# Where the rows of the links and the slot positions are loaded in a two-layer graph kernel

## The reference

```python
src = concatenate([src0, arange(n)]); dst = concatenate([dst0, arange(n)])
h = x @ w_in + b_in
for l in range(2):
    xn = layernorm(h, ln1_g[l], ln1_b[l])
    q, k, v = (xn @ w[l] + b[l] for w, b in ((wq, bq), (wk, bk), (wv, bv)))   # 8 heads of 32
    scores = einsum("ehd,ehd->eh", q[dst], k[src]) * 32 ** -0.5
    ex = exp(scores - segment_max(scores, dst)[dst])
    attn = ex / segment_sum(ex, dst)[dst]
    agg = segment_sum(attn[:, :, None] * v[src], dst)
    h = h + agg @ wo[l] + bo[l]
    h = h + gelu(layernorm(h, ln2_g[l], ln2_b[l]) @ w1[l] + b1[l]) @ w2[l] + b2[l]
x = x + h                                  # h was computed from layernorm(x)
# then: route the mean token to 2 of 8 experts, x = x + layernorm(experts(layernorm(x)) + layernorm(x))
```

## Time and profile before

| | us |
|---|---|
| median of 3 runs | 3951.3 |
| lowest, highest | 3948.37, 3951.6 |
| the profiled execution, its own time | 3945.3 |
| its span | 3943.5 |
| TensorE busy | 2343.8 (59%) |
| VectorE busy | 2487.8 (63%) |
| GpSimd busy | 1835.6 (47%) |

### The profile page before, as it was taken

One profiled execution on the slowest core, in us unless ns is written; L12 is line 12 of the kernel. 1 busy time (PEld: TensorE's weight loads), 2 busy tenths in 40 slices (PEclk: granted clock), 3 DMA queues, 4 the chain that ended last, 5 costly groups with the idle time before them and its releaser, 6 DMA issues. The chain is left out here.

```text
span 3943.5 us, 37530 instructions
## 1 busy us (share of the span) xinstructions
PE 2343.8 (59%) x7257; PEld 1553.1 (39%) x7258; DVE 2487.8 (63%) x3969; ACT 1326.8 (34%) x3895; POOL 1835.6 (47%) x1938
## 2 busy tenths in 40 slices
PE   5763455555455555568882555545555555478798
PEld 3331333333233333345551333333333333256576
DVE  3653677787777777734333777777777877544433
ACT  1112344444344343312112443444444434222131
POOL 4005566666666666311006666666666666211000
PEclk8776676666766676679995766676776666689899
DMA  3225667677677666522216767667666766412111
GB/s 91 64 69 175 186 206 210 203 212 213 201 210 209 207 205 205 154 63 78 72 53 192 211 203 213 205 203 209 207 210 204 212 208 211 118 54 66 39 37 33
DMA packets 293357, 623.34 MB, mean 158 GB/s; under 512 B 51905, under 2 KB 163705, under 8 KB 293184
## 3 DMA queue, kind: packets, MB, share of 16 engines
q0 software_dynamic: 149904, 471.38, 40.8%
q1 hardware_dynamic: 143280, 150.27, 12.0%
HBM read 526.62 MB, written 94.78 MB: 158 GB/s over the span
## 5 line engine op out<-in xcount | busy, mean ns | idle before, releaser
L725 POOL DMA_INDIRECT ring<-kv_table,stage_ix x1760 | 1672.9, 951 | 987.9 <-issue 591.4
L951 PE MATMUL bank<-qs,hot_q 128*128 x1760 | 716.2, 555 | 638.3 <-issue 328.0
L964 PE MATMUL bank<-ring,hot_w 128*128 128x272 f32 x1760 | 704.3, 540 | 501.8 <-issue 295.6
L1860 DVE TENSOR_TENSOR ring<-ring,bank 128x1024 f32<-128x1024 f32 x440 | 532.6, 1210 | 548.9 <-issue 309.5
L951 PEld LDWEIGHTS bank<-qs,hot_q 128*128 128x128 f32 x1760 | 462.4, 275 | 819.9 <-issue 723.9
L964 PEld LDWEIGHTS bank<-ring,hot_w 128*128 128x128 f32 x1760 | 421.1, 259 | 768.5 <-issue 494.4
L1865 DVE TENSOR_REDUCE s<-ring 128x32 f32<-128x1024 f32 x440 | 532.8, 1211 | 4.2
L1210 ACT ACTIVATE stage_o<-bank 128x272 f32<-128x272 f32 x440 | 167.3, 385 | 507.4 <-remote 334.5
L1195 ACT ACTIVATE s<-bank 128x8 f32<-128x8 f32 x440 | 78.0, 177 | 728.5 <-remote 449.1
L1185 ACT ACTIVATE hot_q<-pos_b,row_of 128x128 f32<-128x128 bf16 x880 | 304.0, 395 | 6.8 <-issue 3.4
L1877 DVE TENSOR_TENSOR bank<-ring,bank 128x512 f32<-128x512 f32 x440 | 300.9, 684 | 0.0
(11 more groups left out here) (298 smaller groups left out, 2348.7 us busy)
## 6 DMA issues: line engine op xcount, KB each, us to landing
agg_d<-stage_o SPq DMA_DIRECT2D x440, 136.0 KB
ring<-kv_table,stage_ix POOLq DMA_INDIRECT x1760
pos_b<-rel_d SPq DMA_DIRECT2D x54, 256.0 KB
kv_table<-ring SPq DMA_DIRECT2D x50, 250.0 KB
h_dram<-ring SPq DMA_DIRECT2D x15, 625.0 KB
ring<-h_dram SPq DMA_DIRECT2D x15, 625.0 KB
q_tab<-ring SPq DMA_DIRECT2D x10, 644.5 KB
ring<-in_x_dram SPq DMA_DIRECT2D x10, 625.0 KB
```

Source lines behind the costliest of these rows:

```text
L725: gps.indirect_dma_start(out=chunk[:, par * G + i, j, :], out_offset=None, in_=table, in_offset=bass.IndirectOffsetOnAxis(ap=stage_ix[:, p ...
L951: mm = ten.matmul(q_bank(third, i)[:, 0:QC], hot_q[:, i % 4, a * P:(a + 1) * P], qs[:, bass.ds(t * QC + a * QC, QC)], start=(a == 0), stop ...
L964: mm = ten.matmul(b_acc[i % 2][:, lo - OWN:MC], hot_w[:, i % 4, :], chunk[:, s, j, lo:ROW], start=(j == 0), stop=(j == QD // 2 - 1), skip_ ...
L1860: tt(k_, k_, q, ALU.mult).then_inc(S["q_used"], 1)
```

## The change

Three things are moved, all on SyncE, and nothing else is altered:

- behind `edges(0)` the first rows (`firsts(0)`, with its four waits) are loaded ahead of the 16 weight loads instead of behind them;
- behind `edges(1)` the same with `firsts(1)` and the 8 weight loads;
- the positions of groups 0 and 1 for layer 1 are no longer loaded behind `edges(0)`, but at the beginning of SyncE's last batch of the middle stage.

```diff
--- before.py
+++ after.py
@@ -524,6 +524,9 @@
 
                 def batch(it, last, p):
 
+                    if last and kind == "mid":
+                        for x in range(2):
+                            positions(x, x, G)
                     if not last:
                         hold(sp, s["tok"], o.turn1(it) + 1, S["sp_passed"])
                         load_vh(it + 1)
@@ -586,10 +589,6 @@
             kv_out = kv_table
             dense("in")
             edges(0)
-            sp.wait_ge(S["edges_over"], 1)
-            for x in range(2):
-                positions(x, x, G)
-            load_w("mid", 0)
             kv_in, kv_out = kv_table, kv_table2
 
             def firsts(layer):
@@ -597,13 +596,15 @@
                     sp.wait_ge(S[f"agg_out{i}"], (layer + 1) * (NB // 4) * 16)
                 sp.dma_start(l_first, agg_d[0:NB * P, :].rearrange("(a b e) c -> b a e c", a=2, e=P)[:, :, P - 1, :]).then_inc(S["l_in"], 16)
 
+            sp.wait_ge(S["edges_over"], 1)
             firsts(0)
+            load_w("mid", 0)
             staggered("mid")
             kv_in = kv_table2
             edges(1)
             sp.wait_ge(S["edges_over"], 2)
+            firsts(1)
             load_w("last", 1)
-            firsts(1)
             sp.dma_start(w_qkv[:, 0, 0:2 * NEXP].rearrange("p (a n) -> p a n", a=2), A["L0_ffn_Wr"].rearrange("(a p) n -> p a n", p=P)).then_inc(S["gate_in"], 16)
             sp.dma_start(row_qkv[0:1, 0:NEXP], A["L0_ffn_br"].rearrange("(a n) -> a n", a=1)).then_inc(S["gate_in"], 16)
             sp.dma_start(row_qkv[0:1, D:2 * D], A["L0_ffn_gamma"].rearrange("(a n) -> a n", a=1)).then_inc(S["gate_in"], 16)
```

## The result

| | before | after |
|---|---|---|
| median of 5 runs, us | 3951.6 | 3932.01 |
| lowest, highest | 3948.37, 3959.74 | 3925.7, 3946.72 |
| profiled execution, its own time | 3945.3 | 3932.01 |
| its span | 3943.5 | 3930.1 |

The ratio is 0.995, with a 95% interval of 0.9927 to 0.9974: 10 to 29 us faster. The medians differ by 19.6 us where 20.5 were forecast. The two profiled executions differ by less, 13.4 us in their spans, since that of before happened to be 3 us quicker than the quickest of its timed runs. Where the time came from is read from the pair of profiles, so it has to add up to 13.4.

The account below looks back on a forecast made before the run. Two short gaps behind the edge stages, each a race of three strings meeting at L1729, were held by first rows queued behind weights. Gains 11.4 + 9.2 = 20.6, taken as 20.5, made 3951.3 into 3930.8 us, range 3924 to 3941.

Parts of the forecast that it names:

- Gap one: Stretch behind the first edge stage until L1729 starts the next stage's first batch: 11.4 us gained, bounds 7.6 and 13.0.
- String 1: Links: first rows, home rows, put, copy and gathers ahead of L1729; in gap one to end at 1697.1.
- String 2: Weight loads, then TensorE's and VectorE's folds, ahead of L1729; in gap one to end at 1698.0, at most 1702.2.
- string 3: Loads of the batch's own values and h (L522, L523); in gap one to end last, releasing L1729 at 1698.6.
- The put of gap one: GpSimd's L744 putting the rows back: now lands among the weight loads, 8.3 us instead of 3.9, +4.4.
- Gap two: Stretch behind the second edge stage until L1729: 9.2 us gained, lower bound 0.7, upper bound 11.0.
- The positions: Two loads moved into the middle stage's last batch: cost nothing, or 0.9 us were the cover gone.
- Rival (a): In gap one the fold, at low clock, takes over and ends at 1702.2: 17.0 us gained, 3934.3 us; chance 0.13.
- Rival (b): In both gaps every GpSimd put and gather takes 8.3 us to land: 8.3 us gained, 3943.0 us; chance 0.11.
- Rival (c): Middle stage slower, TensorE's clock staying at 0.50: with 40 us lost, 3970.8 us; chance 0.03.
- Rival (d): Home rows or weights were last all along in the gaps: gain nothing, 3951 us; chance 0.03.
- The signs: Marks expected in the new profile, such as L1971 within 5 us of the edges' end and L1729's wait shrinking.

Follow-up runs that it names:

- e4: Changed kernel with SyncE's first load of x held until GpSimd's gathers of the first batch have landed; 3524.22 us, ratio to before 0.9928.
- e7: e5 with the last stage's weight loads held until the links' gathered home rows are in; 3490.12 us, ratio to before 0.9833.
- e1: Kernel before with only the positions moved into the last batch of the middle stage; 3545.93 us, ratio to before 1.0001.
- e2: Kernel before with only layer 0's first rows loaded ahead of positions and weights; 3538.18 us, ratio to before 0.9978.
- e5: e4 with every load of v and h cut into pieces of 112 and 13 partitions; 3491.0 us, ratio to before 0.9832.
- e8: e6 and e7 together, with 28 added products waiting for the home rows, and x and 125-partition bias loads cut too; 3483.68 us, ratio to before 0.9815.
- after_again: Changed kernel, unaltered, run again on a second chip; 3531.91 us, ratio to before 0.9946.
- e6: e5 with TensorE doing 8 unused identity products ahead of the middle stage's fold; 3491.37 us, ratio to before 0.9842.

## Why the prediction was right, and where it was not

The total came out as forecast, 19.6 us against 20.5, and so did the direction in both gaps and the string that ended each. The terms did less well than the sum. The gaps gave 15.5 us where 20.6 were forecast; that the medians lie so near the forecast is luck, within an interval of the ratio that allows 10 to 29.

- **Gap one, 11.4 forecast, 11.2 measured, in part by luck.** The strings ended in the forecast order. String 1 was not last: the DMA share is back at 0.35, the level of v and h alone, in the stretch from 1692 to 1694, where 1697.1 was forecast for the last gather. String 2 ended at 1697.1, forecast 1698.0; string 3 released L1730 at 1698.69, forecast 1698.6. The put went out at 1673.92, forecast 1674.6. String 3 sets the gap, and its time came out of two errors that cancelled. L522 went out at 1678.21, 2.4 us earlier than before and not 1.5 later: SyncE got past the four waits at 1661.3, and the weights took it 16.5 us to issue instead of 18.5. But from there to the head it took 20.5 us, where the forecast has 16.5. Beside v and h ran the put and all five gathers, whose issues end at 1689.5; in the kernel before only the put ran beside them (the gathers were issued from 1699.7 on, when the stretches show no load any more). That they slowed v and h fits this, but no run separates it. Two smaller errors cancelled in string 2: TensorE's fold took 9.05 us (1684.00 to 1693.05), forecast 8.2, before 6.2; and the weights were in 1.4 us earlier than forecast (1684.00, not 1685.4), partly because SyncE passed the four waits at 1661.3 and not with GpSimd, whose L741 starts at 1662.44.
- **The put of gap one** was charged 4.4 us for landing under the weights, and landed in 4.79 us instead of 3.93, 0.9 more. One microsecond of the charge was a misreading: the 6.9 to 9.3 us of the earlier trace rows count from the start of a gather's issue, as L741's 9.65 us from 3399.33 to 3408.98 show, and were set against 3.9 and 3.0 us that count from the end of one. It cost the forecast nothing, as string 1 was not last.
- **The first rows** landed within 3.7 us of their issue (1661.32 to 1665.05), between the bounds zero and 6.3.
- **Gap two, 9.2 forecast, 4.4 measured: this is the term that was mis-sized.** "L740's second gather ... + 8.3 + 1.8 gives L744" at 14.0 us after the edges' end: it was 15.4, as the gather took 9.65 us. And "from L744 to L1729 18.7 us" was carried over from before, and was 22.5: the put's landing 0.6 more, the gathers' issue 0.4 more, the last gather's landing 2.8 more (6.0 against 3.1). The prediction had named that price as its lower bound and set it aside because "the put would land near 3425, when the weights are in or nearly so". The weights were in (the fold started at 3413.79), but x was not. Counted from the edges' end, v, h and x went out as late as before (L522 at 15.5 us, before 14.9), while the last gather came forward by 7.2 us, and so ran beside x. e4 gives 2.0 of it back by holding x; e7 a further 3.8 by holding the weights.
- **The positions: nothing, as forecast**, with the 26 us of cover that the earlier trace rows showed. That their absence from gap one would be worth 1.4 to 3.3 us (e1, e2) was in the forecast only as "a microsecond or two for us".
- **Rival (a)**, the fold last at a low clock, did not happen in the changed kernel, but by a margin of 1.6 us only; in e5 it did, once string 3 was shortened. **Rival (b)** fell as a whole, as GpSimd waited no more than 4.79 us for gap one's put, yet its mechanism is what took half of gap two. Counted from the end of its issue, the last gather lands in 3.1 to 3.2 us when x is not being loaded and in 6.0 when it is; counted from the start of its issue, the second gather of the home rows lands in 3.05 us with no weight load beside it (e7) and in 8.3 and 9.65 under the weights. **Rival (c)** fell: the middle stage ran at a mean clock of 0.92, as before, and was 1.5 us longer, within what the untouched stages differ by. **Rival (d)** fell with the first wait of L1972.
- **The signs.** Two of those named did not come out. L1972 starts 5.9 us after the edges' end in gap one and 5.3 in gap two, where 5 were allowed; and gap two's wait ahead of the head fell only from 14.49 to 10.96 us and is still for the gathered rows.
- The prediction weighed a rule of the Trainium skill (DMA: Bandwidth & Descriptors, section "Why a DMA increments its semaphore by 16 and not by 1"): 125 partitions use 5 engines. e5 tests it from the other side. The same bytes cut so that 112 partitions stand in one piece ran at 233 GB/s instead of 116, at a share of 1.12 instead of 0.33, as that rule says. The cut also doubles the number of loads, and no run doubles that without changing the partition counts. Against this rival stands that v, h and x, three loads issued one behind the other, were at a share of 0.33 in the changed kernel.

What stays open: what slowed v and h in gap one of the changed kernel, how much of e5's late weights is due to the pieces of v and h, and which of e8's changes gave its gap one.

## What to carry to other kernels

When a stall is taken out of one string of a race, read off when the others end before claiming its length: here a put that goes out 17.8 us earlier became a gain of 11.2. A duration read from a trace holds for its neighbours of that time; if a string moves forward by 10 us, ask which transfers it will now run beside, and price it with the row that had such neighbours. And where the DMA share stands at a third for long, look at the partition counts of the loads: cutting 125 into 112 and 13 took 35 us (e5 against e4) to 39 us (against after_again) out of the two dense stages, nearly twice what this change brought.

## What the runs showed of the hardware that was not expected

- Two chips run the same program 11% apart. The changed kernel's edge stages take 1329 and 1328 us on the first chip and 1129 and 1129 on the chip of after_again, and nothing else differs by more than a few microseconds. GpSimd's L726, 1760 gathers of 0.95 us, shows what its engine waited for ahead of it. On the first chip:

```profile
  remote: 314.8, 93
```

In after_again there is no such row. "remote" stands for a releaser that the profile doesn't name. It explains 315 of the 400 us by its size; its cause is open.
- The fold's 16 products with one column (L824, 32 records) took 6.99 us in gap two at a granted clock of 0.50 (1.2 GHz), after 8.67 us in which TensorE was idle, and 3.63 in e6 (L826), at a granted clock of 1.00 (2.4 GHz) and right behind other products.
- A gather of 110 rows took 3.05 us from the start of its issue to its consumer with no weight load beside it (e7, with the first rows being loaded) and 9.65 beside weight loads.
